# A strided adjacency piece: four runs of 2 KB a partition in place of one of 8 KB

## The chip, the cores and the metric

The kernel runs on one core of one Trainium2 chip. The metric is the time of one execution on the device, in microseconds (us), as the median of several runs.

## What is computed

Two graph layers over 8192 nodes with 128 features. `adj` is an 8192 x 8192 matrix of int32 zeros and ones, about one in 1024 of them a one (some 8 edges a row). Cut to what matters:

```
h = relu(layernorm(x));  x = x + layer0(h, adj)
h = relu(layernorm(x));  x = x + layer1(h, adj)

layer0: att = softmax(where(adj > 0, cos(K, Q), -9e15)) over a row
        out = 0.5 * (att @ h) + 0.5 * h         (h alone where a row has no edge)
layer1: g = h @ W.T + b_W;  e = leaky(g@a1 [row] + g@a2 [column] + b_a)
        out = softmax(where(adj > 0, e, -9e15)) @ g
```

The adjacency matrix is 268 MB. Everything else that is read or written is small beside it.

## The kernel before

The kernel reads the adjacency matrix once, turns each row into a short list of the columns that hold a one, and does both layers by gathering the neighbours' rows from tables in DRAM.

**Tiles and pieces.** 128 rows are a tile; there are 64 tiles (T). A tile is 128 partitions x 8192 int32, 32 KB a partition. It is loaded in four pieces (PIECES = 4) of PIECE = 2048 columns, 8 KB a partition and 1 MB in all. A row's 8192 columns are seen as 16 blocks (BITS) of 512 columns (WORDS), 2 KB each; a piece holds four of them (PIECE_BITS). The pieces go into a ring of six buffers (RING = 6). `load_piece` (L208 to L210) issues one on SyncE's queue (SP). Piece m is number f = m % 4 of tile t = m // 4.

**Folding.** For each of the 16 blocks TensorE multiplies the low byte of the block's 512 integers, read as fp8, by a diagonal matrix `fold[:, b, :]` that holds a power of two of its own for that block, and adds all of them up in one PSUM bank (`folds`, L1021 to L1033; the matmul is L1030, with four matmuls a piece). What comes out for each of 512 word positions is a number with bit b set where block b holds an edge there. The bit is given by the index into `fold`, and the sum doesn't depend on the order of the blocks. After the four matmuls of a piece TensorE raises `piece_folded`; SyncE waits for it before it loads the piece that goes into the same buffer (L957), so six pieces at most are under way.

**The stages, in order of time.**

- Prologue (about 0 to 173 us): `x` is loaded in eight DMAs (L214; 512 B runs), normalised, projected and stored as table `tab0` in 16 DMAs of ScalarE's queue (`store`, L1141; rows of 520 B). ScalarE's `relu` for block b (L1116) waits until the store of block b - 8 has landed, since they share a buffer. In between, the first eight tiles are folded. GpSimd's first gather waits for the last of the stores (L978).
- Main loop (about 173 to 838 us): one turn a tile. TensorE folds tile t + 7 and does the small matmuls of the tiles behind it. VectorE takes the 16 largest words of each half (`extract`), decodes them into column numbers and writes the list; GpSimd issues nine indirect DMAs a tile (L986), each of which gathers 128 rows of 520 B; VectorE and ScalarE turn them into scores (L1364, L1367, L1154), and TensorE sums the weighted rows (L1061). GpSimd may gather tile t only after the weighted sum of tile t - 5 (five buffers).
- Rest of the first layer (about 838 to 917 us): no adjacency is left; GpSimd gathers the last seven tiles, nine gathers each.
- Second layer (about 951 to 1655 us): the lists are there, the adjacency isn't read again. GpSimd issues 544 gathers (L566, L571), followed closely by the other engines.

SyncE's queue issues strictly in the order of the program: x block 0, the weights, x blocks 1 to 3, adjacency pieces 0 to 5, x blocks 4 to 7, then the remaining pieces, each after its wait. All queues share the core's 16 DMA engines.

Of the kernel before, what the change touches and what calls it, by code (L numbers as in the profile page):

```python
# [46 lines left out]
def adjacency_layers(nc, x, adj, wq, wk, w, b_w, a_vec, b_a, out):  # L47
# [11 lines left out]
    WORDS = N // BITS  # L59
# [25 lines left out]
    RING, PIECE_BITS = 6, 4  # L85
    PIECE, PIECES = PIECE_BITS * WORDS, BITS // PIECE_BITS
# [7 lines left out]
    adj_t = adj.rearrange("(t p) c -> t p c", p=P)  # L94
# [7 lines left out]
    with ctx:  # L102
        def sb(name, shape, dt=fp32):
            return ctx.enter_context(nc.sbuf_tensor(name, shape, dt))

        def sem(name):
            return ctx.enter_context(nc.semaphore(name))
# [5 lines left out]
        fold = sb("fold", [P, BITS, P], bf16)  # L113
# [34 lines left out]
        ring_i = [r.bitcast(i32) for r in ring]  # L148
# [42 lines left out]
        keys_ps = ps[0:2]  # L191
# [13 lines left out]
        s_adj = [sem(f"adj_loaded_{r}") for r in range(RING)]  # L205
        s_piece = sem("piece_folded")

        def load_piece(sp, m):  # L208
            t, f = m // PIECES, m % PIECES
            sp.dma_start(ring_i[m % RING], adj_t[t, :, f * PIECE:(f + 1) * PIECE]).then_inc(s_adj[m % RING], 16)  # L210

        def loads_sync(sp):
            def load_x(b):
                sp.dma_start(res[:, 8 * b:8 * b + 8, :], x_t[:, 8 * b:8 * b + 8, :]).then_inc(s_x[b], 16)  # L214

            load_x(0)
            for k, m in enumerate((wq, wk, w)):
                sp.dma_start(wraw[:, k * D:(k + 1) * D], m).then_inc(s_w, 16)
            sp.dma_start(avec[:, 0:1], a_vec[D:2 * D].rearrange("(p o) -> p o", o=1)).then_inc(s_w, 16)
            sp.dma_start(avec[:, 1:2], a_vec[0:D].rearrange("(p o) -> p o", o=1)).then_inc(s_w, 16)  # L220
            sp.dma_start(bcol[:, :], b_w.rearrange("(p o) -> p o", o=1)).then_inc(s_w, 16)
            sp.dma_start(brow[:, 0:D], b_w.rearrange("(o p) -> o p", o=1)).then_inc(s_w, 16)
            sp.dma_start(brow[:, D:D + 1], b_a.rearrange("(o p) -> o p", o=1)).then_inc(s_w, 16)
            for b in range(1, 4):
                load_x(b)
            for m in range(RING):
                load_piece(sp, m)
            for b in range(4, 8):
                load_x(b)
            sp.wait_ge(s_edged, 1)  # L230
            for p, tab in enumerate((tab0, tab1)):
                sp.dma_start(tab[0:1, :], edge_row[:, p, :]).then_inc(s_edge, 16)
# [719 lines left out]
        with nc.Block() as block:  # L952
            @block.sync
            def _(sp):
                loads_sync(sp)
                for m in range(RING, PIECES * T):
                    sp.wait_ge(s_piece, m - RING + 1)  # L957
                    load_piece(sp, m)
                sp.wait_ge(s_edge, 32)
                either(sp, rows_sync, lists_sync)  # L960
# [32 lines left out]
            def _(pe):  # L993
# [27 lines left out]
                def folds(t, first=0, end=PIECES):  # L1021
                    if first == 0:
                        if t >= 2:
                            pe.wait_ge(s_free, t - 1)
                        nc.tensor.matmul(keys_ps[t % 2], ones16[:, :], word_at[:, :], start=True, stop=False)
                    for f in range(first, end):
                        m = PIECES * t + f
                        pe.wait_ge(s_adj[m % RING], 16 * (m // RING + 1))
                        for b in range(PIECE_BITS):
                            last = nc.tensor.matmul(keys_ps[t % 2], fold[:, PIECE_BITS * f + b, :],  # L1030
                                                    ring8[m % RING][:, b * WORDS:(b + 1) * WORDS],
                                                    start=False, stop=PIECE_BITS * f + b == BITS - 1)
                        last.then_inc(s_piece, 1)  # L1033
# [32 lines left out]
                for b in range(NB):  # L1066
                    if b + 1 < NB:
                        transposes(b + 1)
                    if b in early:
                        if b == early[0]:  # L1070
                            pe.wait_ge(s_cdve, MADE)
                            pe.wait_ge(s_const, CONSTANTS)
                        folds(early.index(b))
                    if b == NB - 1:
                        offsets(off0_ps, 0, LEAD)
                    project(b)
                pe.wait_ge(s_sq, 2 * NB)
                pe.wait_ge(s_kc, NB)
                for t in range(-1, LAST):
                    if t + 1 < T:  # L1080
                        owners(t + 1)
                    scan = t + AHEAD + 1
                    if AHEAD + 2 <= scan < T:
                        folds(scan, 0, PIECES // 2)
                    if t == 61:
                        offsets1_tensor(pe)
                    if t == T:
                        pe.wait_ge(s_miss, 1)
                        nc.tensor.matmul(keys_ps[0][0:1, 0:P], st[:, 4:5], ident[:, :], start=True,
                                         stop=True).then_inc(s_flagT, 1)  # L1090
                    if 0 <= t - 4 < T:
                        weighted(t - 4)
                    pair = (t + AHEAD - 3) // 2
                    if t % 2 and LEAD <= pair < PAIRS:
                        offsets(off_ps, pair, 1)
                    if t in (T, T + 1):
                        owners1_tensor(pe, 2 * (t - T))
                        owners1_tensor(pe, 2 * (t - T) + 1)
                    if t % 2 and 0 <= t - 9 < T:
                        second.tensor_tr(pe, (t - 9) // 2)  # L1100
                    if t % 2 == 0 and 0 <= t - 10 < T:
                        second.tensor_pr(pe, (t - 10) // 2)
                    if AHEAD + 2 <= scan < T:
                        folds(scan, PIECES // 2, PIECES)
# [388 lines left out]
```

## Time and profile before

| | us |
|---|---|
| median of 3 runs | 1658.68 (1654.31 to 1660.15) |
| the profiled execution's own time | 1657.38 |
| its span, first to last instruction | 1655.5 |
| around the span | 1.9 |

| engine | busy us | share of the span |
|---|---|---|
| TensorE matmul | 1139.6 | 69% |
| VectorE | 1044.7 | 63% |
| ScalarE | 883.8 | 53% |
| GpSimd | 1131.8 | 68% |

No engine is busy for more than 70% of the span, so the averages name no bound. The profile has to be read by stage: the line of the DMA engines' share has two levels, one for each half of the kernel, and the stages above are cut where it or the work changes.

### The profile page before, as it was taken

To read this page: it belongs to the slowest core of one execution; us is meant where nothing else is said; L and a number is where in the kernel's file an instruction comes from. 1 tells how busy PE (TensorE), PEld (TensorE's weight loads), DVE (VectorE), ACT (ScalarE), POOL (GpSimd) and SP (SyncE) were. 2 spreads that over 40 slices of the span, in tenths; PEclk is the share of its full clock that TensorE was granted. 3 is DMA by queue.
4 is the path that set the end of the run, shared out by engine and by line. 5 is a ranking of instruction groups with operands and counts; after the bars stand their busy time and mean duration, and the time that the engine had idled before them with its cause. 6 is when DMAs were issued, how large, how long until landed. Compare 5 with 4: busy or idle time off the path is not lost. (4 is left out here: it accounts for less than half of the span.)

```text
span 1655.5 us, 22719 instructions
## 1 busy us (share of the span) xinstructions
PE 1139.6 (69%) x6321; PEld 895.3 (54%) x6321; DVE 1044.7 (63%) x4029; ACT 883.8 (53%) x2774; POOL 1131.8 (68%) x1170
## 2 busy tenths in 40 slices
PE   5884677777776767767664576676766666667766
PEld 3552343444444444545454575666766666666765
DVE  6874788888878787888775434444444444444444
ACT  4552455655655565565576364555555555555433
POOL 1236777777767676777777177777777777777775
PEclk9997789888889797888977668778777888787777
DMA  9997999999999999999922122222222222222222
GB/s 328 399 342 247 386 399 399 398 400 400 399 386 399 379 398 377 390 397 386 389 62 60 28 55 59 59 59 59 60 58 60 60 60 59 59 60 59 59 60 47
DMA packets 108397, 361.71 MB, mean 218 GB/s; under 512 B 24421, under 2 KB 57576, under 8 KB 75496
## 3 DMA queue, kind: packets, MB, share of 16 engines
q1 hardware_dynamic: 55272, 277.05, 42.6%
q0 software_dynamic: 35840, 74.62, 17.6%
q10 hardware_dynamic: 17152, 8.52, 2.0%
q8 instruction: 53, 0.87, 0.2%
q14 instruction: 80, 0.66, 0.1%
HBM read 347.38 MB, written 12.72 MB: 218 GB/s over the span
## 5 line engine op out<-in xcount | busy, mean ns | idle before, releaser
L986 POOL DMA_INDIRECT arena<-tab,idx_all x576 | 568.6, 987 | 214.7 <-issue 157.9
L1030 PE MATMUL ps<-arena,fold 128*128 128x512 fp8e4 x1024 | 304.5, 433 | 162.4 <-DMA arena<-in_adj_dram 162.0
L571 POOL DMA_INDIRECT arena<-tab,idx_all x320 | 311.2, 973 | 97.5 <-issue 97.2
L566 POOL DMA_INDIRECT arena<-tab,idx_all x224 | 213.7, 954 | 102.5 <-issue 68.0
L1030 PEld LDWEIGHTS ps<-arena,fold 128*128 128x128 bf16 x1024 | 92.6, 103 | 326.5 <-DMA arena<-in_adj_dram 221.3
L1154 ACT ACTIVATE prod<-prod,arena 128x128 f32<-128x128 f32 x576 | 222.5, 391 | 0.7 <-DVE prod L1364 0.7
L705 DVE SCALAR_TENSOR_TENSOR arena<-ps,s_all,arena 128x512 f32<-128x512 f32 (+1 forms) x112 | 66.8, 632 | 226.6 <-PE ps L587 226.6
L643 ACT ACTIVATE arena<-arena,negm 128x517 f32<-128x517 f32 (+1 forms) x64 | 56.8, 887 | 217.4 <-DVE negm L715 217.4
L529 PE MATMUL ps<-arena 128*128 128x26 f32 x704 | 104.1, 298 | 94.9 <-ACT keys L538 81.0
L587 PE MATMUL ps<-ident,arena 128*128 128x128 f32 x704 | 131.2, 354 | 53.6 <-DMA arena<-tab,idx_all 53.6
L611 PE MATMUL ps<-arena,diag 128*128 128x130 f32 x640 | 110.6, 332 | 82.1 <-issue 78.0
L529 PEld LDWEIGHTS ps<-arena 128*128 128x128 f32 x704 | 102.7, 228 | 98.6 <-ACT arena L520 88.0
L611 PEld LDWEIGHTS ps<-arena,diag 128*128 128x128 f32 x640 | 97.6, 235 | 99.8 <-issue 99.8
L587 PEld LDWEIGHTS ps<-ident,arena 128*128 128x128 f32 x704 | 117.0, 255 | 57.3 <-DMA arena<-tab,idx_all 57.3
L1061 PE MATMUL ps<-arena,diag 128*128 128x130 f32 x768 | 122.6, 322 | 0.0
L1147 ACT COPY arena<-ps 128x462 f32<-128x462 f32 x64 | 34.6, 542 | 163.1 <-PE ps L1049 163.0
L1049 PE MATMUL ps<-arena,R 128*128 128x154 f32 x384 | 72.4, 332 | 71.4 <-DVE R L1343 71.4
L1165 ACT ACTIVATE diag<-ident,weight 128x128 f32<-128x128 f32 x384 | 119.2, 389 | 2.1
L1061 PEld LDWEIGHTS ps<-arena,diag 128*128 128x128 f32 x768 | 119.9, 241 | 0.0
L611 PE MATMUL ps<-arena 128*128 128x130 f32 x704 | 112.5, 321 | 0.0
L636 ACT COPY arena<-ps 128x512 f32<-128x512 f32 (+1 forms) x112 | 50.2, 493 | 114.2 <-issue 78.8
L1049 PEld LDWEIGHTS ps<-arena,R 128*128 128x128 f32 x384 | 64.1, 214 | 86.4 <-DVE R L1343 76.8
(204 smaller groups left out, 2331.3 us busy)
## 6 DMA issues: line engine op xcount, KB each, us to landing
arena<-in_adj_dram SPq DMA_DIRECT2D x256, 1024.0 KB, 15.5
arena<-tab,idx_all POOLq DMA_INDIRECT x1120, 2.6
tab<-arena ACTq DMA_DIRECT2D x16, 260.0 KB, 12.1
tab<-tw ACTq DMA_DIRECT2D x32, 130.0 KB, 10.6
res<-in_x_dram SPq DMA_DIRECT2D x8, 512.0 KB, 7.2
out_dram<-arena SPq DMA_DIRECT2D x64, 64.0 KB, 1.5
prod<-in_L_gnn_Wq_dram SPq DMA_DIRECT2D x1, 64.0 KB
prod<-in_L_gnn_Wk_dram SPq DMA_DIRECT2D x1, 64.0 KB
```

The costliest lines, as they stand in the source:

```text
L529: last = nc.tensor.matmul(rows1_ps[:, c * (S + 2):(c + 1) * (S + 2)], R1[t % 4][:, (c - first) * P:(c - first + 1) * P], owner[:, t, CODE: ...
L566: pool.indirect_dma_start(out=GS[h % 2][:, c, :], out_offset=None, in_=tab1, in_offset=bass.IndirectOffsetOnAxis(ap=idx_all[:, at, slot:sl ...
L571: pool.indirect_dma_start(out=GO[q][:, s, :], out_offset=None, in_=tab1, in_offset=bass.IndirectOffsetOnAxis(ap=idx_all[:, t, s:s + 1], ax ...
L587: last = nc.tensor.matmul(T_ps[c // 4][:, c % 4 * P:(c % 4 + 1) * P], GS[h % 2][:, first + c, D:D + 1].to_broadcast([P, P]), ident[:, :], ...
L611: last = nc.tensor.matmul(out_ps[p][:, 0:ROW], lhs, rhs, start=s == 0, stop=s == K1 + n - 1)
L705: last = nc.vector.scalar_tensor_tensor(out=sc[p][:, a:a + w], in0=T_ps[b][:, 0:w], scalar=s1, in1=m[:, 4 * b * P:4 * b * P + w], op0=ALU. ...
L986: pool.indirect_dma_start(out=G[q][:, s, :], out_offset=None, in_=tab0, in_offset=bass.IndirectOffsetOnAxis(ap=idx_all[:, t, s:s + 1], axi ...
L1030: last = nc.tensor.matmul(keys_ps[t % 2], fold[:, PIECE_BITS * f + b, :], ring8[m % RING][:, b * WORDS:(b + 1) * WORDS], start=False, stop ...
L1049: last = nc.tensor.matmul(E_ps[p][:, c * REC:(c + 1) * REC], R[p][:, c * P:(c + 1) * P], owner[:, t, :], start=True, stop=True)
L1061: last = nc.tensor.matmul(pv_ps[p][:, 0:ROW], lhs, G[q][:, s, :], start=s == K, stop=s == K - 1)
L1154: last = nc.scalar.activation(prod[p][:, s, :], prod[p][:, s, :], ACT.Copy, scale=G[q][:, s, RN:RN + 1], accum_out=score[p][:, s:s + 1])
L1165: last = nc.scalar.activation(diag[t % DR][:, s, :], ident[:, :], ACT.Copy, scale=weight[p][:, s:s + 1])
```

## The change

Piece f of a tile no longer holds the neighbouring blocks 4f to 4f + 3 but the blocks f, f + 4, f + 8 and f + 12. In DRAM that is four runs of 2 KB a partition, 8 KB apart, where it was one run of 8 KB. In the buffer the four blocks lie side by side as before. TensorE takes the matrix of the block that it now finds there: `fold[:, 4b + f, :]` in place of `fold[:, 4f + b, :]`. The number of DMAs (256), their 1 MB each, the number of matmuls and every wait stay.

```
@@ load_piece
         def load_piece(sp, m):
             t, f = m // PIECES, m % PIECES
-            sp.dma_start(ring_i[m % RING], adj_t[t, :, f * PIECE:(f + 1) * PIECE]).then_inc(s_adj[m % RING], 16)
+
+            sp.dma_start(ring_i[m % RING].rearrange("p (b c) -> p b c", c=WORDS),
+                         adj_t[t].rearrange("p (b f c) -> p f b c", f=PIECES, c=WORDS)[:, f, :, :]).then_inc(s_adj[m % RING], 16)
@@ folds
                         for b in range(PIECE_BITS):
-                            last = nc.tensor.matmul(keys_ps[t % 2], fold[:, PIECE_BITS * f + b, :],
+                            last = nc.tensor.matmul(keys_ps[t % 2], fold[:, PIECES * b + f, :],
                                                     ring8[m % RING][:, b * WORDS:(b + 1) * WORDS],
                                                     start=False, stop=PIECE_BITS * f + b == BITS - 1)
```

## Rows read from the trace of the kernel before

**Rows 1.** The page: share of the DMA engines and GB/s in 40 slices.
```profile
DMA  9997999999999999999922122222222222222222
GB/s 328 399 342 247 386 399 399 398 400 400 399 386 399 379 398 377 390 397 386 389 62 60 28 55 59 59 59 59 60 58 60 60 60 59 59 60 59 59 60 47
```

**Rows 2.** Busy time by stage: engines, then TensorE's granted clock, DMA share, GB/s.
```profile
core 0: us, PE busy (x) PEld busy (x) DVE busy (x) ACT busy (x) POOL busy (x), PEclk, DMA share, GB/s
0.00:124.00 124.00, 93.64 (x464) 63.61 (x465) 89.13 (x411) 63.54 (x157) 31.99 (x45) 0.93 0.97 357
124.00:173.00 49.00, 19.52 (x74) 10.67 (x72) 23.46 (x78) 10.72 (x35) 30.71 (x32) 0.72 0.81 262
173.00:838.00 665.00, 486.42 (x2388) 310.16 (x2388) 547.34 (x2441) 383.44 (x1602) 484.01 (x490) 0.86 1.00 388
838.00:917.00 79.00, 39.11 (x212) 36.37 (x210) 47.60 (x212) 54.75 (x235) 60.23 (x62) 0.74 0.28 60
917.00:1655.00 738.00, 500.96 (x3188) 474.54 (x3188) 337.12 (x891) 371.39 (x747) 524.89 (x544) 0.77 0.25 57
```

**Rows 3.** Waits, 173 to 838 us: who waited for whom; total us, times, longest.
```profile
PEld ps L1030 <- DMA arena<-in_adj_dram: 209.7, 129, 3.9
PE ps L1030 <- DMA arena<-in_adj_dram: 153.5, 110, 3.4
POOL arena L986 <- issue: 133.8, 439, 0.3
...
POOL arena L986 <- PE ps L1061: 38.7, 22, 4.1
```

**Rows 4.** DMA queues, 173 to 838 us: packets, MB, share of 16 engines; issues to landing.
```profile
q1 hardware_dynamic: 30446, 221.64, 83.5%
q0 software_dynamic: 15716, 32.70, 14.8%
q10 hardware_dynamic: 6256, 3.06, 1.6%
...
arena<-in_adj_dram SPq DMA_DIRECT2D x210, 1024.0 KB, 16.5
```

**Rows 5.** DMA, 16 to 26 us: adjacency pieces alone, 8 KB packets.
```profile
DMA packets 578, 4.21 MB, mean 421 GB/s; under 512 B 64, under 2 KB 64, under 8 KB 64
...
q1 hardware_dynamic: 578, 4.21, 101.4%
```

**Rows 6.** DMA, 30 to 34 us: loads of x alone, 512 B packets.
```profile
DMA packets 2237, 1.15 MB, mean 288 GB/s; under 512 B 34, under 2 KB 2235, under 8 KB 2235
...
q1 hardware_dynamic: 2236, 1.14, 109.2%
```

**Rows 7.** DMA, 60 to 80 us: adjacency pieces (q1) beside the stores of tab0 (q10).
```profile
q1 hardware_dynamic: 955, 6.95, 88.0%
q10 hardware_dynamic: 1592, 0.80, 13.8%
```

**Rows 8.** Waits, 0 to 140 us; the last row is from the whole run.
```profile
ACT arena L1116 <- issue: 18.3, 5, 5.4
...
PE ps L999 <- ACT arena L1116: 14.9, 5, 5.0
...
PE ps L1030 <- DMA arena<-in_adj_dram: 8.6, 5, 5.5
...
POOL arena L986 <- DMA tab<-arena: 7.5, 1, 7.5
```

**Rows 9.** Timeline, VectorE, 150 to 170 us: its first waits for gathers, in brackets.
```profile
153.86 0.96 DVE L1364 TENSOR_TENSOR prod<-arena 128x768 f32<-128x768 f32 x1 [14.01 <-DMA arena<-tab,idx_all]
156.83 0.56 DVE L1367 TENSOR_TENSOR prod<-arena 128x384 f32<-128x384 f32 x1 [2.01 <-DMA arena<-tab,idx_all]
...
169.09 0.56 DVE L1367 TENSOR_TENSOR prod<-arena 128x384 f32<-128x384 f32 x1 [4.25 <-DMA arena<-tab,idx_all]
```

**Rows 10.** Gathers of the first layer (L986): times of start, and waits before them.
```profile
L986 POOL DMA_INDIRECT arena<-tab,idx_all x576: 938/944/1930, 141.0 to 915.9; - x192
```

**Rows 11.** Timeline, GpSimd and TensorE, where the adjacency stream ends.
```profile
836.37 1.00 POOL L986 DMA_INDIRECT arena<-tab,idx_all  x1 [2.06 <-PE ps L1061]
...
831.38 1.83 PE L1030 MATMUL ps<-arena,fold 128*128 128x512 fp8e4 x4 [2.02 <-DMA arena<-in_adj_dram]
...
836.38 1.97 PE L1030 MATMUL ps<-arena,fold 128*128 128x512 fp8e4 x8
```

**Rows 12.** The page: DMA issues of the stores of tab0, median us to landing.
```profile
tab<-arena ACTq DMA_DIRECT2D x16, 260.0 KB, 12.1
```

More of the change, by code:

```diff
@@ L209, in load_piece @@
             t, f = m // PIECES, m % PIECES
-            sp.dma_start(ring_i[m % RING], adj_t[t, :, f * PIECE:(f + 1) * PIECE]).then_inc(s_adj[m % RING], 16)
+            sp.dma_start(ring_i[m % RING].rearrange("p (b c) -> p b c", c=WORDS),
+                         adj_t[t].rearrange("p (b f c) -> p f b c", f=PIECES, c=WORDS)[:, f, :, :]).then_inc(s_adj[m % RING], 16)
         def loads_sync(sp):
@@ L1029, in folds @@
                         for b in range(PIECE_BITS):
-                            last = nc.tensor.matmul(keys_ps[t % 2], fold[:, PIECE_BITS * f + b, :],
+                            last = nc.tensor.matmul(keys_ps[t % 2], fold[:, PIECES * b + f, :],
                                                     ring8[m % RING][:, b * WORDS:(b + 1) * WORDS],
```

## Prediction, made before the changed kernel was run

> **What bounds the kernel now.** I read the page's DMA line first, since the change touches a transfer. It has two levels: nearly all of the 16 DMA engines' time is taken in the first half at some 400 GB/s, and a quarter or less in the second at some 60 [rows 1]. So I cut the run into stages [rows 2]. From 173 to 838 us the share is 1.00, while TensorE is busy for 486 of 665 us, VectorE for 547 and GpSimd for 484. The waits of that stage name the same thing: TensorE's fold, L1030, is what waits for the adjacency pieces, 153.5 us of matmul time [rows 3]. A piece takes 16.5 us from issue to landing [rows 4]: six pieces are under way, and 665 us by 210 pieces is 3.17 us a piece, so the queue is nearly always full. The main loop runs at the speed of the DMA engines. The one engine near it is GpSimd: 490 gathers, busy 484.01 us, with 133.8 us of issue time between them, leave 47 us of 665 [rows 2, 3]. It is second, and a slower stream gives it more room. After 838 us nothing of the adjacency matrix is read, and the DMA share is 0.28 and 0.25 [rows 2]; there the change does nothing.
>
> **What the change removes and adds.** It removes nothing and adds no instruction. It reads the same bytes in four times as many packets. The profile counts one packet for one contiguous run: in the stretch with adjacency alone, 578 packets less 64 small ones (the semaphore writes) carry 4.21 MB, 8192 B each [rows 5]. So 256 pieces x 128 partitions = 32,768 packets of 8 KB become 131,072 of 2 KB. TensorE's matmuls keep their count and shape and read another slice of `fold`, already in SBUF: nothing. SyncE issues as many DMAs; each has to be made into 512 packets rather than 128, and loads of x are made into 1024 with packets leaving at 560 a us [rows 6], three times the 188 a us that 2 KB packets would need at 385 GB/s: nothing either.
>
> **The price of a 2 KB packet.** The trace has none in this stream, but has the ends on both sides, from the same queue and in the same direction. 8 KB: 514 packets in 10 us on 16 engines, 160 / 514 = 311.3 ns each [rows 5]. 512 B: 2,202 packets in 4 us, 64 / 2202 = 29.1 ns each [rows 6]. If a packet costs a fixed part and a part by bytes, the byte part is (311.3 - 29.1) / 7680 = 36.7 ps a byte and the fixed part 29.1 - 18.8 = 10.3 ns. A 2 KB packet then takes 10.3 + 75.2 = 85.5 ns, four take 342.1 ns, and what was one packet costs 30.8 ns more (9.9%; the stream alone would fall from 421 to 383 GB/s). Bounds: nothing at all, if the 512 B packets are held back by something that a 2 KB packet no longer feels; and 3 x 29.1 = 87.3 ns, if each added packet cost a whole 512 B one. I take the line between the two rows, since 2 KB lies between them. Against it speaks that 520 B stores beside the 8 KB packets cost little: 1.67 times as many small packets as large ones, and the two shares add up to 1.02, as in the pure stretch [rows 7, 5]; but those go the other way, into DRAM.
>
> The 512 B stretch ran at 288 GB/s and the 8 KB stretch at 421 [rows 5, 6]. The Trainium skill (DMA: Bandwidth & Descriptors, Specifications) has 512 B as the least transfer for line rate; by that rule the price would be zero and the time that of the third rival below. The trace disagrees with it. The same page (section on the iDMA fabric) gives 408.7 GB/s for a load stream with 4 KiB rows; no run here shows 4 KB, but the line above gives 16 x 4096 / 160.8 ns = 407.6, so they agree.
>
> **The sum.** A piece is 128 packets on 16 engines, 8 each: 8 x 30.8 = 246 ns more.
>
> Main loop: 210 pieces x 0.246 = +51.7 us, all on the path. The share is 1.00 where the saturated stretches have 1.01 to 1.02 [rows 2, 5], so up to 2% of 665 us, 13 us, was not fully used and could take part of it; I keep that for the range, since the gaps are short and the added work is everywhere.
>
> Prologue, the other 46 pieces: 46 x 0.246 = 11.3 us more DMA work before 173 us. The share of 124 to 173 us is 0.81, which is 9 to 10 us not used [rows 2], and TensorE waited only 8.6 us for pieces up to 140 us [rows 8]. What set this stage from 140 us on was a chain of small transfers: GpSimd waited 7.5 us for the last store of `tab0` [rows 8], started its gathers at 141.0 [rows 10], and VectorE waited 14.0, 2.0 and 4.25 us for what they brought [rows 9]. Before that ScalarE stood 18.3 us at L1116, where it waits for an older store, and TensorE 14.9 us behind it [rows 8]. These stores and gathers share the engines with the stream and take turns with it by the packet. A store is 512 packets, 32 an engine. With a turn of 311 ns between two of its packets it needs some 10 us, with a turn of 85 ns some 3. So the small transfers get through earlier, and the pieces later. I take a gain of 5 us at the last store, 3 at the first gathers, a loss of 3 where the stream itself holds up a fold: -5 us, between -12 (the ScalarE waits go too) and +7 (all waits stay and folds come later).
>
> End of the stream to 917 us: the gather at 836.37 us was released by the weighted sum of tile 52, between the halves of tile 63's fold [rows 11], by the program's order and not by the stream's speed. The same seven tiles remain, at GpSimd's own pace: 0. Second layer: 0.
>
> Total +51.7 - 5 = +46.7 us. The profiled execution took 1657.4 (span 1655.5 and 1.9 around it): 1657.4 + 46.7 = 1704.1, and the median is 1.3 above that execution. I forecast **1704 us**, 2.8% above the median. What a measurement of this kernel can tell from no change is about 0.3%, 5 us.
>
> **How else it could go.**
>
> *First rival: a smaller fixed part.* The 512 B packets may be slowed by more than the fixed cost, so that the line overstates it. With a third of it, 3.4 ns, the main loop grows by 210 x 8 x 10.2 ns = 17 us, less 5 in the prologue: 1669 to 1670 us. For it: the small packets of [rows 7] seem cheap. Against: a straight line needs nothing else.
>
> The Trainium skill (same page, Why small descriptors are slow) gives a fixed overhead of about 3 cycles a packet, beside 64 for 2 KB and 256 for 8 KB at 32 bytes each: 268 for 259, +3.5%. Worked out from that, the main loop would be some 18 us longer, which is this rival. At 512 B it makes 19 for 16, while [rows 6] against [rows 5] is 29.1 ns for 19.5 ns by bytes, so the trace has it two to three times as large.
>
> *Second rival: the added packets cost more*, since reads jump by 8 KB in DRAM after each 2 KB and mix with gathers. The bound is 87.3 ns: 210 x 8 x 87.3 = 147 us, 1800 us. With half of it, 1725 us. Against: the loads of x jump by 64 KB after each 512 B and are in the 29.1 ns already.
>
> *Third rival, on the other side: faster.* A 2 KB packet streams as well as an 8 KB one, and only the turn-taking changes. The place is the prologue, 60 to 170 us. The gain there is worked out above, 5 to 12 us: 1646 to 1652, say 1650 us. It decides if a row's extra cost is below 8 us / (210 x 8) = 5 ns, a sixth of my 30.8. For it: the waits of [rows 8, 9] are real. Against: the 32% lower rate of the 512 B stretch. If extra cost and gain balance, the change shows nothing: 1654 to 1663.
>
> *Fourth: the engines take turns by bytes or by DMA*, so that the small transfers gain nothing. That is my forecast without its 5 us: 1709, inside its range.
>
> **How the numbers follow.** Forecast (with the fourth), 1684 to 1722: 0.66. Its low end is the fixed part a quarter smaller and 7 us more in the prologue or covered; its high end has +7 in the prologue and the fixed part a tenth higher. First rival, 1664 to 1684: 0.13. Second, above 1722: 0.06. Third, below 1653: 0.09. Balance: 0.06. The range 1667 to 1724 holds the forecast, most of the first rival and the start of the second, about 0.8. Faster by over 0.3%: 0.09; within: 0.06; slower by over 0.3%: 0.85.
>
> **What would show it.** Right: some 153,000 packets on SyncE's queue; in the first stretch with adjacency alone, about 383 GB/s where it was 421; the main loop some 50 us longer, its DMA share still 1.00 to 1.02, bytes a us about 7% lower; TensorE's wait for pieces at L1030 up by about as much; GpSimd's waits for L1061 up as well; store landings clearly shorter than their median of 12.1 us [rows 12]; the time from the stream's end to the end of the run the same to 2 us. Wrong: the pure stretch at 421 GB/s (third rival) or near 405 (first); or a main loop whose share falls below 1, which would mean that something other than the engines' time, such as SyncE's issue, holds the stream.

## The result and the profile after

The changed kernel takes 1700.78 us (median of 4 runs, 1698.37 to 1703.44), the kernel before 1658.22: a ratio of 1.0255, 95% interval 1.023 to 1.028. That is 42.6 us more; the forecast was 1704 us.

The profiled execution took 1703.44 us, its span is 1701.6 us, 46.1 longer than before. (It was the longest of the four; the profiled execution of the kernel before lay 0.8 us below its median. So the stages below add up to 46.1 and not to 42.6.) The page's share of the DMA engines and GB/s in 40 slices, to be read against [rows 1]:

```profile
DMA  9997999999999999999962112222222222222222
GB/s 313 385 389 239 371 371 372 374 368 365 369 367 363 367 364 371 361 370 370 358 223 59 37 46 57 59 58 59 60 59 59 60 60 59 57 60 59 59 60 48
```

The upper level has sunk from about 395 to about 370 GB/s and the engines are as full as before. The stages of the changed kernel, in the columns of [rows 2]:

```profile
0.00:124.00 124.00, 94.73 (x464) 65.93 (x465) 88.92 (x411) 63.87 (x157) 32.06 (x45) 0.93 1.03 361
124.00:170.00 46.00, 19.41 (x74) 10.74 (x72) 23.93 (x76) 10.45 (x35) 30.21 (x31) 0.75 0.80 250
170.00:881.00 711.00, 499.83 (x2391) 318.65 (x2391) 551.15 (x2444) 384.75 (x1602) 488.37 (x492) 0.85 1.03 364
881.00:958.00 77.00, 39.41 (x209) 36.82 (x207) 46.52 (x210) 54.62 (x234) 58.71 (x61) 0.68 0.28 58
```

To cut the runs at the same place of the program, I take the first matmul of tile 10's fold and the end of the last fold. From TensorE's timeline of the kernel before (start, duration, what; in brackets the wait ahead of it):

```profile
173.11 3.38 PE L1030 MATMUL ps<-arena,fold 128*128 128x512 fp8e4 x8
```

and of the changed kernel:

```profile
170.39 3.59 PE L1032 MATMUL ps<-arena,fold 128*128 128x512 fp8e4 x8
...
879.72 1.08 PE L1032 MATMUL ps<-arena,fold 128*128 128x512 fp8e4 x4 [0.61 <-DMA arena<-in_adj_dram]
```

Before, the main loop goes from 173.1 to 836.38 + 1.97 = 838.35 [rows 11]: 665.2 us. After, from 170.4 to 880.8: 710.4 us. So the 46.1 us of span are: prologue -2.7, main loop +45.2, the rest of the run 817.2 to 820.8, +3.6.

The price shows undisturbed in the first stretch with adjacency alone. Changed kernel, 16 to 26 us, DMA packets and SyncE's queue, against [rows 5]:

```profile
DMA packets 1951, 3.87 MB, mean 387 GB/s; under 512 B 63, under 2 KB 63, under 8 KB 1951
...
q1 hardware_dynamic: 1951, 3.87, 104.4%
```

1951 - 63 = 1888 packets in 160 us of engine time: 84.7 ns each, 339.0 ns for four, where one of 8 KB took 311.3. That is 27.7 ns more a row, or 9.2 ns for each added packet. In the main loop, 45.2 us over 210 pieces x 8 rows an engine is 26.9 ns. TensorE's waits of the main loop (170 to 881 us), against [rows 3]:

```profile
PE ps L1032 <- DMA arena<-in_adj_dram: 197.8, 137, 3.3
...
POOL arena L988 <- issue: 128.6, 422, 0.3
...
POOL arena L988 <- PE ps L1063: 84.5, 38, 5.4
```

TensorE waits 44.3 us longer for pieces (153.5 before) and GpSimd 45.8 us longer for a free buffer (38.7 before): on both engines the addition stands as idle time behind the stream. The prologue (0 to 140 us), against [rows 8]:

```profile
PE ps L1032 <- DMA arena<-in_adj_dram: 17.3, 8, 5.5
...
PE ps L1001 <- ACT arena L1118: 5.5, 2, 5.0
POOL arena L988 <- DVE idx_all L1356: 5.3, 1, 5.3
```

ScalarE's 18.3 us of waits for older stores are no longer among the waits, and GpSimd's 7.5 us for the last store neither; TensorE's waits for pieces have doubled from 8.6 to 17.3 us. The stores land sooner, as the page's list of DMA issues shows. The kernel before, beside [rows 12]:

```profile
tab<-tw ACTq DMA_DIRECT2D x32, 130.0 KB, 10.6
```

and the changed kernel:

```profile
tab<-arena ACTq DMA_DIRECT2D x16, 260.0 KB, 8.5
tab<-tw ACTq DMA_DIRECT2D x32, 130.0 KB, 6.5
```

The second kind are the stores of the second layer's table, made in the main loop and behind it.

### The profile page after: what moved, and what is told of

It is laid out like the page before. It is cut to its first block and busy times, and to the rows that moved or that the text cites. A ratio compares the mean times of both kernels' runs of the same rounds, so it can differ in the third digit from the quotient of the medians.

```text
span 1701.6 us, 22719 instructions
## 1 busy us (share of the span) xinstructions
PE 1161.0 (68%) x6321; PEld 913.3 (54%) x6321; DVE 1047.8 (62%) x4029; ACT 885.7 (52%) x2774; POOL 1137.3 (67%) x1170
## 3 DMA queue, kind: packets, MB, share of 16 engines
q1 hardware_dynamic: 153576, 277.05, 45.9%
## 5 line engine op out<-in xcount | busy, mean ns | idle before, releaser
L1032 PE MATMUL ps<-arena,fold 128*128 128x512 fp8e4 x1024 | 310.2, 435 | 218.2 <-DMA arena<-in_adj_dram 215.1
L613 PE MATMUL ps<-arena,diag 128*128 128x130 f32 x640 | 112.2, 336 | 77.0 <-issue 73.3
L531 PEld LDWEIGHTS ps<-arena 128*128 128x128 f32 x704 | 105.0, 233 | 97.5 <-ACT arena L522 87.0
L613 PEld LDWEIGHTS ps<-arena,diag 128*128 128x128 f32 x640 | 99.1, 238 | 94.9 <-issue 94.9
L1063 PE MATMUL ps<-arena,diag 128*128 128x130 f32 x768 | 128.0, 331 | 0.0
L1063 PEld LDWEIGHTS ps<-arena,diag 128*128 128x128 f32 x768 | 126.1, 252 | 0.0
L613 PEld LDWEIGHTS ps<-arena 128*128 128x128 f32 x704 | 110.9, 242 | 0.0
```

Of the source, the lines that this page charges most:

```text
L531: last = nc.tensor.matmul(rows1_ps[:, c * (S + 2):(c + 1) * (S + 2)], R1[t % 4][:, (c - first) * P:(c - first + 1) * P], owner[:, t, CODE: ...
L613: last = nc.tensor.matmul(out_ps[p][:, 0:ROW], lhs, rhs, start=s == 0, stop=s == K1 + n - 1)
L1032: last = nc.tensor.matmul(keys_ps[t % 2], fold[:, PIECES * b + f, :], ring8[m % RING][:, b * WORDS:(b + 1) * WORDS], start=False, stop=PIE ...
L1063: last = nc.tensor.matmul(pv_ps[p][:, 0:ROW], lhs, G[q][:, s, :], start=s == K, stop=s == K - 1)
```

## The experiments

### Is it the packet, or the place in DRAM?

The change does two things at once: it makes packets of 2 KB, and it makes the reads of a row jump. `near2k` does the first alone. Two buffers are interleaved in SBUF, so that a piece of neighbouring blocks goes into slots of 2 KB with gaps between them. In DRAM each row is still one run of 8 KB. (Cut to the load; the fold matmul reads its block from the same slots.)

```
-        ring = [take(PIECE) for _ in range(RING)]
+        pairs_of_pieces = [take(2 * PIECE) for _ in range(RING // 2)]
+        RUN = WORDS
-        ring_i = [r.bitcast(i32) for r in ring]
+        ring_i = [pairs_of_pieces[r // 2].bitcast(i32).rearrange("p (k q c) -> p k q c", q=2, c=RUN)[:, :, r % 2, :]
+                  for r in range(RING)]
-            sp.dma_start(ring_i[m % RING], adj_t[t, :, f * PIECE:(f + 1) * PIECE])...
+            sp.dma_start(ring_i[m % RING], adj_t[t, :, f * PIECE:(f + 1) * PIECE].rearrange("p (k c) -> p k c", c=RUN))...
```

> Pieces of four neighbouring blocks as in the kernel before, so 8 KB in one place of DRAM, but laid into the buffers with gaps of 2 KB (two buffers interleaved), so that each row goes in four packets of 2 KB. Theory 1 (a fixed cost for each packet): as the changed kernel, 387 GB/s in the pure stretch and 1700 us. Theory 2 (the 8 KB jumps in DRAM cost): as the kernel before, 421 GB/s and 1658 us. Half of each would be 1679 us.

Measured: 1699.28 us, ratio 1.0246 (1.0215 to 1.0277), the changed kernel's time. Its stretch from 16 to 26 us:

```profile
DMA packets 1951, 3.87 MB, mean 387 GB/s; under 512 B 63, under 2 KB 63, under 8 KB 1951
```

The same count to the packet. Its main loop took 707.5 us, from 169.9 to 877.4, where the changed kernel's took 710.4. That is one trace each, and the medians are 1.5 us apart with overlapping runs, so jumps cost 3 us at most, which these runs can't tell from nothing; the packets are the price. Nor does it matter which side of the copy is in pieces: here it is the SBUF side alone, in the changed kernel the DRAM side alone.

`near1k` is the same with `RUN = HALF`: slots of 1 KB, eight packets a row; each fold matmul reads its block as two halves.

> As the kernel with neighbouring blocks in 2 KB packets, but in 1 KB packets, eight a row. Theory 1: a 1 KB packet takes 9.2 + 37.8 = 47.0 ns, the pure stretch runs at 349 GB/s, seven added packets a row cost 210 x 8 x 64.7 ns = 109 us in the main loop: 1658 + 109 - 3 = 1764 us. Theory 2: 1658 us. If SyncE's issue or the making of packets became the limit, the DMA share of the main loop would fall below 1 and the time would be over 1764.

Measured: 1771.75 us, ratio 1.0683 (1.065 to 1.0716), 8 us over the forecast of 1764. Its stretch from 16 to 26 us:

```profile
DMA packets 3451, 3.48 MB, mean 348 GB/s; under 512 B 48, under 2 KB 3451, under 8 KB 3451
```

3403 packets, 47.0 ns each, as the line says. The main loop took 770.2 us, 105.0 more than before (62.5 ns a row, 8.9 for each added packet), and its DMA share is 1.07, so nothing but the engines holds it. The miss is in the prologue, forecast 3 us shorter and 8 us longer (the fold of tile 10 at 181.1 us). ScalarE's waits for older stores were already gone with 2 KB, so nothing more was to be had there, while a piece costs 0.52 us more and TensorE's waits for pieces up to 140 us rise to 22.1 us.

`runs4k` goes the other way: the piece is two runs of 4 KB, blocks 2f, 2f + 1, 2f + 8 and 2f + 9.

```
-            sp.dma_start(ring_i[m % RING], adj_t[t, :, f * PIECE:(f + 1) * PIECE])...
+            sp.dma_start(ring_i[m % RING].rearrange("p (h c) -> p h c", h=2),
+                         adj_t[t].rearrange("p (h g c) -> p g h c", h=2, c=2 * WORDS)[:, f, :, :])...
-                            last = nc.tensor.matmul(keys_ps[t % 2], fold[:, PIECE_BITS * f + b, :],
+                            last = nc.tensor.matmul(keys_ps[t % 2], fold[:, BITS // 2 * (b // 2) + 2 * f + b % 2, :],
```

> Pieces of two runs of 4 KB, 16 KB apart. The changed kernel's stretch with adjacency alone gave 84.8 ns for a 2 KB packet, the kernel before 311.3 ns for one of 8 KB: 9.2 ns fixed and 36.9 ps a byte. Theory 1, a fixed cost for each packet: a 4 KB packet takes 160.3 ns, the pure stretch runs at 409 GB/s, one added packet a row costs 210 x 8 x 9.2 ns = 15.5 us in the main loop, less 1 in the prologue: 14 to 15 us above the kernel before, 1673 us. Theory 2, jumps in DRAM cost and packets do not: one jump a row where the change has three, also a third, 14 to 15 us. Theory 3, only packets under some size are slow (2 KB is, 4 KB is not): 421 GB/s and 1655 to 1659 us.

Measured: 1665.48 us, ratio 1.0048 (1.0033 to 1.0062): 7.6 us, half of the forecast loss. The price is there; 16 to 26 us:

```profile
DMA packets 1063, 4.09 MB, mean 409 GB/s; under 512 B 64, under 2 KB 64, under 8 KB 1063
```

999 packets, 160.2 ns each, against 160.3 forecast. The main loop took 677.5 us, +12.3. But the prologue is 7.2 us shorter: the fold of tile 10 starts at 165.95 us. I had allowed for 1 us there, and the next section asks why it was more. (The profiled execution was the fastest of the ten, 3.8 us below the median, so its stages add up to 4.4 us and not to 7.6.)

`runs16k` has pieces of eight blocks, 16 KB a partition, and three buffers (`RING, PIECE_BITS = 3, 8`).

> Pieces of eight neighbouring blocks: 16 KB a partition in one run, 2 MB a DMA, three buffers instead of six, two pieces a tile. Theory 1 (a fixed cost for each packet): half the packets, 4.6 ns less for each 8 KB, 427 GB/s in the pure stretch, 210 x 8 x 4.6 = 8 us less in the main loop. If turns between queues are taken by the packet, stores and gathers wait up to 613 ns for a turn, and the prologue loses 3 to 5 us: 1653 to 1656 us. Rival, the size of the piece hurts: TensorE waits for 2 MB before it can fold, and the small transfers fall behind: 10 us or more slower, 1668 us and over. If long packets are cut in any case: 421 GB/s, 1658 us.

Measured: 1663.28 us, ratio 1.0032 (1.0018 to 1.0045): a little slower, not faster. 16 to 26 us:

```profile
DMA packets 297, 4.34 MB, mean 434 GB/s; under 512 B 32, under 2 KB 32, under 8 KB 32
```

265 packets of 16 KB would be 603.8 ns each, but a stretch of 10 us holds only some 16 of them an engine, and where it is cut matters. From 14 to 26 us it is 313 in 12 us, 613 ns each, as the line says, and 427 GB/s, where the kernel before has 424 in the same stretch. The main loop took only 2.7 us less than before, not 8. Its waits from 172 to 835 us:

```profile
ACT lnv L334 <- DVE mv L326: 206.1, 25, 9.5
PEld ps L1049 <- DVE R L1343: 172.3, 53, 7.4
PE ps L1049 <- DVE R L1343: 144.7, 53, 6.5
```

No row names a wait of TensorE for pieces any more; it waits for VectorE's masks (`R`). After the last fold GpSimd needed 85.3 us to its last gather of the first layer, where it was 77.6: it had fallen behind. That the stream was no longer the bound would explain both, but isn't shown: the DMA share of the main loop is 1.00, as before. The size and number of the pieces changed too, so the loss is not put down to one cause.

### Where the prologue gains

With 2 KB throughout, the prologue was 2.7 us shorter, with 4 KB 7.2 us, with 1 KB 8.0 us longer. Small packets let the stores through, and cost engine time. To separate the two places, the change or its 4 KB form is made for some tiles only, as in

```
+            if t >= 11:        # late2k; t < 11: early2k, early4k; 8 <= t < 11: mid4k; t < 8: first4k
+                ...            # the strided load, and below the matching index into fold
+            else:
                 sp.dma_start(ring_i[m % RING], adj_t[t, :, f * PIECE:(f + 1) * PIECE])...
```

> The change from tile 11 on alone; tiles 0 to 10, the prologue's, are loaded as in the kernel before. Theory (two effects that add): the prologue as before, so the fold of tile 10 starts at about 173 us, and the main loop as in the changed kernel, 45 us longer: 1658 + 45 = 1703 us, 2 to 3 above the changed kernel. Rival (the prologue gains nothing by the small packets): the same as the changed kernel, 1700 us.

> The change in tiles 0 to 10 alone; the main loop is loaded as in the kernel before. Theory: ScalarE's waits for older stores (18 us before, none in the changed kernel) go and TensorE's waits for pieces grow from 9 to 17 us, so that the fold of tile 10 starts at about 170.4 us instead of 173.1; then 665 us as before: 1655 us, 3 less than the kernel before. Rival: the difference in the prologue was chance, or is given back at the start of the main loop: 1658 us.

> Tiles 0 to 10 in two runs of 4 KB, the rest as in the kernel before. Theory: with 4 KB throughout, the fold of tile 10 started at 166.0 us, 7.2 earlier than before, since stores get a turn twice as often and a piece costs only 0.07 us more; then 665 us as before: 1651 us, faster than both kernels. Rival (that start was chance, or GpSimd, next to the bound, gives it back in the main loop): 1655 to 1658 us.

> Tiles 8 to 10 alone in two runs of 4 KB: the pieces that are under way beside the last stores and the first gathers. My prediction put 8 us of gain there, 5 at the last store and 3 at the first gathers. If that is the place, 1652 to 1654 us. If the gain comes from ScalarE's waits for older stores between 60 and 105 us, where tiles 2 to 7 are loaded, nothing is left of it: 1657 to 1658 us.

These four, and two that I repeated for that reason,

> The change from tile 11 on alone, once more, beside a kernel before that takes its usual 1658 us. Theory (two effects that add): the fold of tile 10 starts at about 173 us as before and the main loop is 45 us longer: 1703 us. Rival (the prologue gains nothing by the small packets): as the changed kernel, 1700 us. The two are near each other in time; the start of the fold of tile 10, 173 or 170 us, tells them apart.

> Tiles 0 to 10 in two runs of 4 KB, the rest as in the kernel before, once more, beside a kernel before that takes its usual 1658 us. Theory: the fold of tile 10 starts at about 166 us instead of 173 and the rest is as before: 1651 us. Rival (given back in the main loop, where GpSimd is next to the bound): 1655 to 1658 us.

ran on two chips on which the kernel before itself took 2035.5 and 2007.0 us in place of 1658 (mean granted clock 0.73 to 0.76 where the others have 0.79 to 0.82), so their times are not compared with the others, only with the kernel before beside them: late2k 1.0097 (1.0045 to 1.0148) and again 1.0067 (1.0024 to 1.011); early2k 1.0017 (0.9959 to 1.0075); early4k 0.9991 (0.9927 to 1.0056) and again 0.9946 (0.9899 to 0.9994); mid4k 1.0001 (0.9943 to 1.0059). Only the two of late2k, whose expected effect was 45 us, and by a hair the repeat of early4k exclude 1; for an effect of 3 to 7 us these timings are too coarse.

They tell two other things. First, the engines stood idle there for stretches that no releaser explains; of mid4k's waits from 1000 us on, one row (the same wait was 78.0 us, 62 times, longest 2.9 in the kernel before on its usual chip):

```profile
PE ps L615 <- issue: 353.2, 58, 35.1
```

and in the main loop the stream was not the bound all the time. Stage from 181 to 912 us of mid4k (8 KB packets in this stage but for one tile), columns of [rows 2]:

```profile
181.00:912.00 731.00, 510.55 (x2389) 312.74 (x2388) 546.61 (x2406) 380.21 (x1596) 488.28 (x483) 0.81 0.93 352
```

and of late2k (2 KB packets), 181 to 930 us:

```profile
181.00:930.00 749.00, 526.99 (x2391) 323.91 (x2391) 547.59 (x2407) 381.28 (x1598) 492.07 (x484) 0.80 0.99 344
```

A share of 0.93 rises to 0.99, where full engines with 2 KB packets show 1.03, and the loop is 17 us longer (748.4 for 731.4), not 45. The other traces from these chips say the same: with 8 KB in the main loop it took 729.3 to 737.0 us (early2k, early4k twice), with 2 KB in late2k's repeat 745.3. So the price there was 11 to 19 us, compared on the same chip. The whole kernel became 2.5% longer where the engines were full and 0.7 to 1.0% where they had 7% of slack. What else held the loop on these chips is open.

Second, up to about 165 us their traces run as on the other chips: early4k's fold of tile 9 starts at 153.09 and 152.92 us, runs4k's at 153.07. So that start can be compared. It is at 160.81 us in the kernel before, 158.50 in the changed kernel, 157.89 in early2k, 160.69 and 162.32 in the two late2k. The prologue's gain belongs to the small packets of the prologue. And mid4k places it. Its waits up to 140 us, and its timeline:

```profile
ACT arena L1121 <- issue: 25.5, 6, 8.4
...
POOL arena L990 <- DVE idx_all L1354: 5.0, 1, 5.0
...
159.60 4.75 PE L1035 MATMUL ps<-arena,fold 128*128 128x512 fp8e4 x16
```

The wait for the last store is gone, as with 2 KB, but ScalarE's waits for older stores are still there, and the fold of tile 9 starts 1.2 us earlier than before instead of 7.7. The last two runs, beside a kernel before of 1661.3 us:

> Tiles 0 to 10 in two runs of 4 KB, the rest as in the kernel before, a third time. The fold of tile 9 started at 153.1 and 152.9 us in its two traces, 7.8 us earlier than before. Theory (this is kept to the end): a ratio of 0.995 to the kernel before, 1650 us where the kernel before takes 1658. Rival (given back in the main loop, where GpSimd is next to the bound): 0.998 to 1.000.

Measured: 1655.22 us, ratio 0.9965 (0.9952 to 0.9978). The fold of tile 9 starts at 153.06 us and the last fold ends at 831.6, 6.8 us earlier than before; 0.35 of the forecast 0.5% is kept.

> Tiles 0 to 7 alone in two runs of 4 KB, the complement of the kernel with tiles 8 to 10, whose trace kept 25 us of ScalarE's waits for older stores and had the fold of tile 9 at 159.6 us. Theory (the gain is the end of ScalarE's waits between 60 and 105 us): these waits go, the fold of tile 9 starts at 153 to 155 us, and the time is that of tiles 0 to 10 in 4 KB, a ratio of 0.995 to 0.996. If both places are needed, 157 us and 0.998.

Measured: 1651.97 us, ratio 0.9945 (0.9933 to 0.9957). Its waits up to 140 us, and its timeline:

```profile
ACT arena L1121 <- issue: 3.6, 3, 1.5
...
154.24 4.95 PE L1035 MATMUL ps<-arena,fold 128*128 128x512 fp8e4 x16
...
830.58 1.08 PE L1035 MATMUL ps<-arena,fold 128*128 128x512 fp8e4 x4 [1.39 <-DMA arena<-in_adj_dram]
```

ScalarE's waits are down from 18.3 to 3.6 us, the fold of tile 9 starts 6.6 us earlier, the last fold ends at 831.7, 6.7 us earlier, and the span is 1650.0. With mid4k this places the gain: it lies in tiles 0 to 7, where ScalarE's waits for older stores are. Packets of 4 KB for tiles 0 to 7 and of 8 KB for the rest are faster than the kernel before, by 0.4 to 0.7%, and so than the changed kernel as well. Whether tiles 8 to 10 in 4 KB harm or not is open. The six runs of first4k (1650.49 to 1652.64 us) all lie below the six of early4k_c (1653.60 to 1657.52), so the 3 us between them aren't scatter from run to run. But up to the end of the last fold the two traces are level (831.7 and 831.6 us), and it is behind it, on the same instructions, that early4k_c took 822.3 us and first4k 818.3. I found no cause for that.

## Why the prediction was right, point by point

**The sum.** The forecast was +46.7 us, and the two profiled executions are 46.1 apart. That closeness is partly luck: the main loop came out 6.5 us shorter than forecast, the prologue 2.3 and the rest of the run 3.6 us longer. In the medians it was +42.6. Two slips of arithmetic are in the text too: 1704 is 2.7% above the median of 1658.68, not 2.8%, and with the 1.3 us from the profiled execution to the median the sum is 1705.4.

**What bounds the kernel.** Right. The main loop took nearly the whole price: +45.2 us of 46.5 (210 x 8 x 27.7 ns) that the pure stretch gives. Where the engines had slack, as in late2k, it took less than half. The share came out at 1.03, above the forecast 1.00 to 1.02; the pure stretch rose in step, from 1.01 to 1.04.

**The number of packets.** Right: SyncE's queue has 153,576 packets on the page of the changed kernel; 153,000 were forecast.

**The price of a packet.** The mechanism is right, the size a tenth too large: 30.8 ns a row forecast, 27.7 measured. The step was the fixed part, 10.3 ns from two stretches of [rows 5, 6]; three sizes measured later give 9.0 to 9.3. The stretch of 4 us of 512 B packets [rows 6] was too rough for a difference of a nanosecond: near1k has one of 6 us (31 to 37 us) with 3384 packets, 28.4 ns each instead of 29.1, and the same working with 28.4 gives a fixed part of 9.5 ns and 28.6 ns a row. This one term explains that 51.7 us were forecast for the main loop and 45.2 came. The line itself held from 1 to 8 KB: 47.0, 84.7, 160.2 and 311.3 ns. That reads jump in DRAM was weighed under the second rival, and near2k shows no cost for it.

*The small packets of [rows 7]* were misread as cheap. There 6.95 MB of adjacency are 848 packets of 8 KB, 264 of the 320 us of engine time at 311.3 ns each; what is left, 56 us for 1592 store packets, is 35 ns each, where the line gives 28 for 520 B. By the shares themselves it is 27.7 ns (13.8% of 320 us). So these rows never spoke for the first rival.

The 4 KB stretch ran at 409 GB/s. The Trainium skill (DMA: Bandwidth & Descriptors, section on the iDMA fabric) gives 408.7 for a load stream with 4 KiB rows; the trace agrees. The 512 B for line rate that the same page of the Trainium skill states (Specifications) does not hold here: at 1 KB the stream is at 348 GB/s, at 2 KB at 387.

**SyncE's issue.** Nothing was forecast and nothing showed: even with 1024 packets a piece the DMA share of the main loop stayed at 1.07.

**The prologue.** -5 forecast, -2.7 came, and of its parts two were wrong. *The gain at the last store*, 5 us: the wait of 7.5 us went, but 5.3 us of a wait for VectorE's index lists took its place, and the first gather started at 138.8 us instead of 141.0 [rows 10], a gain of 2.2. *The gain at the first gathers*, 3 us: none. VectorE's first product, changed kernel, against [rows 9]:

```profile
151.75 0.96 DVE L1366 TENSOR_TENSOR prod<-arena 128x768 f32<-128x768 f32 x1 [13.27 <-DMA arena<-tab,idx_all]
```

It starts 12.95 us after the first gather, before 12.9. And *ScalarE's waits*, which I kept for the end of the range, were the main thing: they went in full, and TensorE's waits for pieces took most of it back. With 4 KB they also go but for 2.7 us, and a piece costs 0.07 us more rather than 0.22, so that more remains (TensorE's waits for pieces were 12.7 us up to 140 us). The turn-taking by packets itself is borne out: the stores of `tab0` land after 12.2, 12.1, 10.6, 8.5 and 7.3 us (medians of 16) with packets of 16, 8, 4, 2 and 1 KB in the stream. From 8 to 4 KB that step is within the scatter, since late2k's two traces, with 8 KB there, have 13.6 and 9.2 us. The 32 stores of the main loop show it more clearly: 10.2 to 10.6 us with 8 KB (before, first4k, early4k_c), 7.9 with 4, 6.5 and 6.6 with 2, 5.9 with 1 KB.

**End of the stream and second layer.** 0 forecast, +3.6 in the two traces. That misses the 2 us given as a sign of being right. From the last fold on, seven kernels with the same instructions there and no adjacency left took 816.5 (runs4k), 817.2 (before), 818.3 (first4k), 820.3 to 820.8 (near1k, near2k, changed) and 822.3 (early4k_c); runs16k, whose GpSimd is behind, 828.1. A difference of this size comes without any packets of 2 KB too, and isn't put down to the change.

**The rivals.** None came. The first (a third of the fixed part) and the third (faster) needed a pure stretch near 405 or at 421 GB/s; it was 387. The second had the jumps as its reason, which near2k answers, and the fourth (turns not by packets) is answered by the stores, which land sooner.

## What to carry to other kernels

Where the DMA engines are full, count packets, not only bytes: each contiguous run costs about 9 ns of one engine's time beside its bytes, and a run is broken by either side of the copy. Where small transfers of another queue wait behind a bulk stream, shorter packets in the stream let them through, and this can be worth more than it costs (0.55% here, with 4 KB for the first eight tiles): try it only for the stretch in which they wait. The price of a resource is paid in full only as far as that resource is the bound; read its share in the stage before multiplying.

## What was not expected of the hardware

- A destination with gaps cuts packets just as a source with jumps: near2k and the changed kernel have the same 1951 packets in 10 us, at the same 387 GB/s.
- The share of the DMA engines goes over 1 as packets shrink: 1.01 at 8 KB, 1.02 at 4 KB, 1.04 at 2 KB, about 1.09 at 1 KB (109.5% of near1k's stretch), and 1.09 [rows 6] to 1.15 (near1k, 31 to 37 us) at 512 B. Records of packets overlap, so a share of 1.03 is no more work done than one of 1.00.
- The landing of gathers gained little by short packets in the stream, that of stores much. VectorE's first product came 12.6 to 13.5 us after the first gather in all eight kernels on the usual chips, in no clear order of packet size. In the main loop the landings that the traces have took 7.4 us (median) with packets of 16 KB, 5.9 and 6.1 with 8, 5.7 with 4, 5.5 with 2 and 5.8 with 1 KB. Why the two differ is open.
